# First attention of a two-layer block: projections spread over the slots, maxima turned in the products' bank, output bias as a weight row

## The chip, the cores and the metric

The kernel runs on one core of a Trainium2 chip. The metric is the device time of one execution in microseconds, the median of the runs of a kernel. Engines are called by the profile's names: PE is TensorE (matrix products; PEld its weight loads), DVE is VectorE, ACT is ScalarE, POOL is GpSimd, SP is SyncE, which here issues nearly all DMAs.

## The reference

Two layers, each a cross attention and a feed-forward stage, over 16 batches of 100 tokens of width 256. Only the first attention is touched by the change:

```
def _L0_xattn_ref(query, key_value, Wq, bq, Wk, bk, Wv, bv, Wo, bo):   # 16 heads of 16, 361 keys of width 192
    q = (query @ Wq + bq)       k = (key_value @ Wk + bk)       v = (key_value @ Wv + bv)    # split into heads
    attn = jnp.einsum('bhqd,bhkd->bhqk', q, k) * scale
    attn = jnp.clip(attn, -CLAMP, CLAMP)
    attn = jax.nn.softmax(attn, axis=-1)
    attn = jnp.where(jnp.any(jnp.isnan(attn)), jnp.asarray(1.0 / Nkv, attn.dtype), attn)
    x = jnp.einsum('bhqk,bhkd->bqhd', attn, v).reshape(B, Nq, Cq)
    return x @ Wo + bo
```

Its query is the layer norm of the tokens and its result is added to them. Behind it stand a mixture of experts, a second attention with quantised linears, and a gated cell; they take the rest of the time and stay as they are.

## The kernel before

It is written engine by engine: each engine's program is an order written out by hand, and the engines meet at semaphores. The attention runs batch by batch (`over_batches`: batches 0 and 1 written out, 2 to 11 in a loop of two batches a turn, 12 to 15 written out). A batch `b` is cut into eight slots `i`, one for each pair of heads, and `a_tensor`, `a_scalar`, `a_vector`, `a_gpsimd` give what each engine does in each slot; `a_sync` gives the DMA issues of a batch in their order.

In each slot TensorE does `t_tensor` (L551: the transposed scores of two heads of batch b, keys on the partitions, with the maximum subtracted by two extra rows, plus a floor column; banks 4 and 5), and then `s_tensor` (L532: the plain scores of two heads of batch b+1, banks 0 to 3 in turn). ScalarE takes the exponential of the first (`exp_scalar`, L558); VectorE takes the row maxima of the second (`s_vector`, L537) and clips the probabilities of the slot before (`clip_vector`, L567). Four times a batch `pv_tensor` (L581) multiplies four heads' probabilities by their values into bank 6, `OB_`, columns 0 to 399; a column of ones beside the values gives the softmax's denominator in partition 16 of each group of 32.

Between them lie the steps of later or earlier batches, all through one bank, 7, `UB_`, one after another, each waiting until the one before has been read: `k_tensor` (L379, two parts), `v_tensor` (L477, parts 0 and 1 of 12 and 6 products), `q_tensor` (L413), `y_tensor` (L623, the output product of batch b-2, read by `y_vector`, L633), and `m_tensor` (L506). The last turns eight heads' maxima, trimmed by `m_vector` (L500), so that they lie on rows; `m_scalar` (L512) and `m_low` (L516) split them into a high and a low half-precision part, and `rows_store` (L523) puts both as rows into the queries' tile, which `t_tensor` needs. `k_gpsimd` (L397), `q_gpsimd` (L430, L433) and `c_gpsimd` (L654) make the low parts of K, Q and the context on GpSimd, `on_gpsimd` (L617) scales the products by the inverted denominators. These come back by `inv_load` (L611), a DMA that spreads them over the partitions. `k_store` and `half_load` send K through DRAM into the layout of the scores.

The constant part of the output, bv·Wo + bo, is one row, `ybias`, made in the prologue; `x_bias_gpsimd` (L642) adds it to all tokens on GpSimd, four additions of 100x1024 in batches 0 and 1. Batches 14 and 15 also hold a guard for not-a-number (`guard_...`), whose sums and output product use `UB_` too.

Of the kernel before, what the change touches and what calls it, by code (L numbers as in the profile page):

```python
# [10 lines left out]
ALU = mybir.AluOpType  # L11
# [37 lines left out]
def build(nc, a, out):  # L49
    ctx = ExitStack()  # L50
    with ctx:
# [97 lines left out]
        def bias_row_tensor(pe, part):  # L149

            pe.wait_ge(wvo_in, 32)
            for k in range(2 * part, 2 * part + 2):
                pe.matmul(OB_[0:1, 0:C], bv_col[:, k:k + 1], w_in_["Wo_heads"][0][:, k, :], start=(k == 0), stop=False)
            if part == 1:
                pe.matmul(OB_[0:1, 0:C], ones_row[:, 0:1], bo_row[:, :], start=False, stop=True).then_inc(yb_mm, 1)
# [116 lines left out]
        least = sba("least", [T, H // 2])  # L272
# [13 lines left out]
        UH_ = UB_[:, :].bitcast(F16)  # L286
# [209 lines left out]
        def m_vector(v, b, p, half):  # L496
# [3 lines left out]
            v.scalar_tensor_tensor(m32c[:, :], m32[p][:, half * NP:(half + 1) * NP], CLAMP, least[:, :], ALU.min, ALU.max  # L500
                                   ).then_inc(m_c, 1)

        def m_tensor(pe, b, half, free):
            turn_free(pe, free)
            pe.wait_ge(m_c, 2 * b + half + 1)
            pe.transpose(UB_[0:NP, 0:T], m32c[:, :], ident[0:T, 0:T]).then_inc(m_mm, 1)  # L506

        def m_scalar(s, b, half):
# [3 lines left out]
            s.copy(mT[:, half, 0, :], UB_[0:NP, 0:T]).then_inc(m_h, 1)  # L512

        def m_low(v, b, half):
            v.wait_ge(m_h, 2 * b + half + 1)
            v.tensor_tensor(mT[:, half, 1, :], UB_[0:NP, 0:T], mT[:, half, 0, :], ALU.subtract).then_inc(m_l, 1)  # L516
# [52 lines left out]
        def pv_tensor(pe, b, p, g):  # L569
# [4 lines left out]
            if g == 0 and is_first(b):  # L574
                pe.wait_ge(yb_ev, 2)
# [43 lines left out]
        def y_tensor(pe, b, free):  # L619
            turn_free(pe, free)  # L620
            pe.wait_ge(o_n, b + 1)
            for k in range(HG):
                mm = pe.matmul(UB_[0:T, 0:C], on32[:, k * T:(k + 1) * T], w_in_["Wo_heads"][0][:, k, :], start=(k == 0),  # L623
                               stop=(k == HG - 1))
            mm.then_inc(y_mm0, 1)

        def y_vector(v, b):

            v.wait_ge(y_mm0, b + 1)
            if is_first(b):  # L630
                v.wait_ge(x_bias, LG)
# [29 lines left out]
        def a_tensor(pe, b, t, p):  # L661
            q = 1 - p
            for i in range(NP):
# [10 lines left out]
                if i % 2 and i >= 3:  # L674
                    pv_tensor(pe, b, p, (i - 3) // 2)
                if i == 1 and from_(b, 1):
                    pv_tensor(pe, b - 1, q, NQ - 1)
                if i == 0:
                    m_tensor(pe, b, 1, (k_32, 2 * b + 5) if has(b, 2) else (yb_ev, 3) if has(b, 1) else (y_x, b - 2))
                if i == 1 and has(b, 2):  # L680
                    k_tensor(pe, b + 2, p, 1, (m_l, 2 * b + 2))
                if i in (2, 3) and has(b, 1):
                    v_tensor(pe, b + 1, q, i - 2, (v_ev, 2 * b + 3) if i == 3 else
                             (k_32, 2 * b + 6) if has(b, 2) else (yb_ev, 4))
                if i == 4 and has(b, 1):
                    m_tensor(pe, b + 1, 0, (v_ev, 2 * b + 4))
                if i == 5 and has(b, 3):
                    q_tensor(pe, b + 3, q, (m_l, 2 * b + 3))
                if i == 6 and from_(b, 2):
                    y_tensor(pe, b - 2, (q_32, b + 4) if has(b, 3) else  # L690
                             (m_l, 2 * b + 3) if has(b, 1) else (m_l, 2 * b + 2))
                if i == 7 and has(b, 2) and not has(b, 3):
                    guard_sums_tensor(pe, (y_x, b - 1))
                if i == 1 and has(b, 1) and not has(b, 2):
                    guard_even_tensor(pe, (m_l, 2 * b + 2))
                if i == 7 and has(b, 3):
# [2100 lines left out]
```

## Time and profile before

| | |
|---|---|
| median of 3 runs | 946.31 us (946.12 to 947.51) |
| profiled execution | 947.37 us |
| its span, first to last instruction | 945.5 us |
| TensorE's granted clock, mean | 0.91 |
| busy: PE, DVE, ACT, POOL | 792.7, 708.9, 559.2, 298.9 us |

The profiled execution's own time is the span and what lies around it, 1.9 us. In the rows further down, a time is counted from the span's start. A row of the time order gives start, duration, engine, line, operation, the tile written and the tiles read, shapes, and in brackets the engine's idle time ahead of it with what ended it. Matrix products overlap: the distance between two starts, not the duration, is what one occupies.

### The profile page before, as it was taken

The numbers are of one execution on the slowest core, as the hardware profiler recorded it, in microseconds if no ns is written. First come the engines' busy times: TensorE is split into PE (matmuls) and PEld (weight loads), VectorE is DVE, ScalarE is ACT, GpSimd is POOL, SyncE is SP. The second block draws the span as 40 slices with busy tenths as digits, with TensorE's granted clock in tenths as the row PEclk, the third lists the DMA queues.
The fourth block names the chain that finished last, engine by engine and source line by source line (L and its number), as shares of the span: only waits on it lengthen the run. The fifth ranks groups of instructions, "written<-read, shape, count | busy, mean of one in ns | idle before, by whom it ended". The sixth has DMA issues, their size and how long they took to land.

```text
span 945.5 us, 22076 instructions
## 1 busy us (share of the span) xinstructions
PE 792.7 (84%) x8198; PEld 582.7 (62%) x8198; DVE 708.9 (75%) x1450; ACT 559.2 (59%) x1159; POOL 298.9 (32%) x258
## 2 busy tenths in 40 slices
PE   3777888889898768999889999997655999769994
PEld 2455666666665645777657777784213887459994
DVE  8678777877877888777476666654796998677866
ACT  6666666666665436634365555536897776673542
POOL 6166444444441506040232220002730221342400
PEclk9699999999999776999999999997557999789998
DMA  6423444344452246515076554455210000200002
GB/s 169 108 70 86 113 96 99 103 97 114 119 121 81 80 138 222 175 35 145 23 222 188 170 168 146 124 135 142 75 42 11 1 1 1 90 1 2 2 2 70
DMA packets 76898, 89.53 MB, mean 95 GB/s; under 512 B 22150, under 2 KB 64929, under 8 KB 76826
## 3 DMA queue, kind: packets, MB, share of 16 engines
q1 hardware_dynamic: 69994, 80.50, 30.6%
q0 software_dynamic: 6144, 7.42, 3.0%
q8 instruction: 45, 0.74, 0.3%
q10 hardware_dynamic: 688, 0.66, 0.3%
q14 instruction: 27, 0.22, 0.1%
HBM read 72.87 MB, written 15.43 MB: 93 GB/s over the span
## 4 chain that ended last, share of the span: by engine, by line
PE 53%; DVE 26%; ACT 9%; issue 8%; POOL 2%; DMA 1%; ACTq 0%; DVEq 0%; POOLq 0%
PE ps L1207 11%; PE ps L1194 10%; PE ps L581 4%; PE ps L379 3%; PE ps L477 3%; PE ps L551 3%; DVE p L567 3%; PE ps L623 3%; PE ps L532 2%; PE ps L2229 2%; DVE m L537 2%; PE ps L2240 2%; DVE pmax L1681 1%; ACT area L2039 1%; PE ps L1728 1%
## 5 line engine op out<-in xcount | busy, mean ns | idle before, releaser
L537 DVE TENSOR_REDUCE m<-ps 100x2 f32<-100x722 f32 x128 | 115.6, 904 | 51.6 <-PE ps L532 49.7
L558 ACT ACTIVATE p<-ps 128x800 f32<-128x800 f32 x128 | 106.8, 834 | 41.6 <-PE ps L551 38.6
L1256 ACT ACTIVATE hT<-ps,cols 128x500 f32<-128x500 f32 (+1 forms) x96 | 62.5, 651 | 103.3 <-PE ps L1194 103.1
L1263 DVE TENSOR_TENSOR hT_l<-hT,hT_h 128x500 f16<-128x500 f32 (+1 forms) x96 | 62.4, 652 | 59.1 <-ACT hT_h L1257 59.1
L567 DVE SCALAR_TENSOR_TENSOR p<-p 128x600 f32<-128x600 f32 x128 | 106.6, 834 | 0.0
L1207 PE MATMUL ps<-w_h,hT_h 128*125 128x256 f16 (+1 forms) x384 | 104.7, 273 | 1.8 <-DVE x L1303 1.2
L1207 PE MATMUL ps<-w_h,hT_l 128*125 128x256 f16 (+1 forms) x384 | 104.7, 273 | 0.0
L1207 PE MATMUL ps<-w_l,hT_h 128*125 128x256 f16 (+1 forms) x384 | 104.7, 273 | 0.0
L1099 POOL DMA_INDIRECT xe<-tokens,slot_of x32 | 43.2, 1349 | 151.4 <-PE ps L1217 102.1
L1194 PE MATMUL ps<-xe_h,w_h 128*128 128x500 f16 (+1 forms) x192 | 73.3, 382 | 15.8 <-DVE xe_l L1237 5.5
L551 PE MATMUL ps<-qs,ks 128*128 128x100 f16 x768 | 63.3, 212 | 14.7 <-ACT p L558 14.7
L1194 PE MATMUL ps<-xe_l,w_h 128*128 128x500 f16 (+1 forms) x192 | 73.0, 380 | 0.0
L1194 PE MATMUL ps<-xe_h,w_l 128*128 128x500 f16 (+1 forms) x192 | 72.6, 378 | 0.0
L551 PEld LDWEIGHTS ps<-qs,ks 128*128 128x128 f16 x768 | 51.1, 100 | 28.2 <-ACT p L558 20.1
L532 PE MATMUL ps<-ks,qs 128*100 128x361 f16 x256 | 62.9, 330 | 3.5 <-DMA qs<-q_parts 3.1
L397 POOL TENSOR_TENSOR kp<-k,kp 128x361 f16<-128x361 f32 x32 | 31.6, 989 | 98.8 <-ACT kp L393 98.8
L1257 ACT ACTIVATE hT_h<-ps,cols 128x500 f16<-128x500 f32 (+1 forms) x96 | 62.1, 647 | 0.0
L581 PE MATMUL ps<-p,v 128*32 128x100 f32 (+1 forms) x1536 | 48.7, 262 | 8.3 <-DVE p L567 8.0
L1207 PEld LDWEIGHTS ps<-w_h,hT_h 128*125 128x125 f16 (+1 forms) x384 | 50.9, 132 | 6.3 <-DVE hT_l L1263 1.4
L1207 PEld LDWEIGHTS ps<-w_l,hT_h 128*125 128x125 f16 (+1 forms) x384 | 50.9, 133 | 2.7
L1207 PEld LDWEIGHTS ps<-w_h,hT_l 128*125 128x125 f16 (+1 forms) x384 | 50.9, 133 | 0.0
L551 PE MATMUL ps<-qs,floor_k 128*128 128x100 f16 x256 | 50.7, 212 | 0.0
(348 smaller groups left out, 2101.6 us busy)
## 6 DMA issues: line engine op xcount, KB each, us to landing
sw<-in_L_ffn_w_dram SPq DMA_DIRECT2D x16, 512.0 KB, 6.8
sw<-in_L_ffn_w_dram SPq DMA_DIRECT2D x8, 1024.0 KB, 5.8
k_parts<-kp SPq DMA_DIRECT2D x32, 192.0 KB, 2.2
ks<-k_parts SPq DMA_DIRECT2D x32, 192.0 KB
stage<-in_L_xattn_W_f_dram SPq DMA_DIRECT2D x6, 1024.0 KB, 7.5
ctx_f<-in_ctxT_dram SPq DMA_DIRECT2D x16, 270.8 KB, 3.2
stage<-in_ctxT_dram SPq DMA_DIRECT2D x8, 541.5 KB, 8.6
area<-in_ctxT_dram SPq DMA_DIRECT2D x16, 270.8 KB, 6.1
```

Of the source, the lines that this page charges most:

```text
L532: mm = pe.matmul(bank[at + n][0:T, 0:KV], qs[p][:, h, :], ks[p][:, h, 0:KV], start=True, stop=True)
L537: v.tensor_reduce(m32[p][:, 2 * i:2 * i + 2], ps[0:T, at:at + 2, 0:KV], AX.X, ALU.max).then_inc(m_max, 1)
L551: mm = pe.matmul(bank[t_bank(i) + n][:, j * T:(j + 1) * T], keys, qs[p][:, h, :], start=(j == 0), stop=True, skip_group_check=True)
L558: s.activation(p32[:, i % HALF, :, :, :].rearrange("p j n t -> p n j t"), ps[:, t_bank(i):t_bank(i) + 2, 0:(KJ + 1) * T].rearrange("p n (j ...
L567: v.scalar_tensor_tensor(probs, probs, 1.0, low, ALU.min, ALU.max).then_inc(a_cv, 1)
L581: i = pe.matmul(OB_[HR * r:HR * (r + 1), g * T:(g + 1) * T], v32[p][0:m, j, h, :], p32[0:m, h // 2 % HALF, j, h % 2, :], start=(g == 0 and ...
L1099: g.indirect_dma_start(xe[e % 2][:, j, :], None, x_d, bass.IndirectOffsetOnAxis(ap=slot_of[:, 4 * e + j:4 * e + j + 1], axis=0)).then_inc( ...
L1194: i = pe.matmul(bank[2 + f % 2][:, 0:width(n)], w1p[ww][:, k, f * 128:(f + 1) * 128], xep[p][xx][:, k, 0:width(n)], start=(k == 0 and ww = ...
L1207: i = pe.matmul(bank[4 + j % 3][0:m, 0:C], hTp[p][hh][:, f, j * m:(j + 1) * m], w2p[of][ww][:, f, :], start=(f == 0 and hh == ww), stop=(f ...
L1256: s.activation(hT[:, f % 3, 0:m], bank[2 + f % 2][:, 0:m], ACT.Silu, bias=bias, scale=1.0 / WS)
L1257: s.activation(hTp[p][0][:, f, 0:m], bank[2 + f % 2][:, 0:m], ACT.Silu, bias=bias, scale=1.0 / WS).then_inc(f_s, 1)
L1263: v.tensor_tensor(hTp[p][1][:, f, 0:m], hT[:, f % 3, 0:m], hTp[p][0][:, f, 0:m], ALU.subtract).then_inc(f_l, 1)
```

## The change

- `over_batches` writes out batches 0 to 3 and loops over 4 to 11.
- K part 0 of batch b+2 moves from slot 7 of batch b-1 to slot 0 of batch b; V part 0 from slot 2 to 1, K part 1 from 1 to 2, Q from 5 to 4; V part 1 stays in slot 3; Y is cut in two halves, in slots 6 and 7; PV moves behind them in its slots. ScalarE's and GpSimd's orders follow.
- The maxima are turned into `MT_`, 100 columns of the products' bank behind the products, and no longer wait for `UB_`; instead TensorE waits for the maxima's low part (`m_l`) before the next PV.
- `ybias` is stored by a DMA from SyncE as row 16 of the output weight of head 0, where the denominator times its inverse, one, meets it. The additions on GpSimd go.
- On SyncE, the store of K part 1 comes after the loads of the next half, just before the maxima rows of batch b+1.
- In the prologue, Q of batch 2 moves up to slot 0, and the bias rows turn in `UB_`.
- The lower bound `least` of the trimming is one column, broadcast.

```diff
-        UH_ = UB_[:, :].bitcast(F16)
+        MT_ = OB_[0:H // 2, HG * T:(HG + 1) * T]
...
-            v.scalar_tensor_tensor(m32c[:, :], m32[p][:, half * NP:(half + 1) * NP], CLAMP, least[:, :], ALU.min, ALU.max
+            v.scalar_tensor_tensor(m32c[:, :], m32[p][:, half * NP:(half + 1) * NP], CLAMP, least[:, :].broadcast_to((T, NP)), ALU.min,
+                                   ALU.max
...
-        def m_tensor(pe, b, half, free):
-            turn_free(pe, free)
+        def m_tensor(pe, b, half):
             pe.wait_ge(m_c, 2 * b + half + 1)
-            pe.transpose(UB_[0:NP, 0:T], m32c[:, :], ident[0:T, 0:T]).then_inc(m_mm, 1)
+            pe.transpose(MT_, m32c[:, :], ident[0:T, 0:T]).then_inc(m_mm, 1)
...
-        def x_bias_gpsimd(g, n):
-            g.wait_ge(yb_ev, 2)
-            g.wait_ge(ln_xn, LB * (n + 1))
-            part = x[:, LB * n:LB * (n + 1), :]
-            g.tensor_tensor(part, part, ybias_b[:, None, :].broadcast_to((T, LB, C)), ALU.add).then_inc(x_bias, 1)
+        def bias_row_store(sp):
+
+            sp.wait_ge(yb_ev, 1)
+            sp.dma_start(w_in_["Wo_heads"][0][D:D + 1, 0, :], ybias[:, :]).then_inc(wvo_in, 16)
...
 def a_tensor(pe, b, t, p):
-                if i % 2 and i >= 3:
-                    pv_tensor(pe, b, p, (i - 3) // 2)
+                if i == 0:
+                    m_tensor(pe, b, 1)
+                if i == 0 and has(b, 2):
+                    k_tensor(pe, b + 2, p, 0, (y_x, b - 2) if from_(b, 3) else (q_32, b + 3) if from_(b, 1) else (yb_ev, 2))
+                if i == 1 and has(b, 2):
+                    v_tensor(pe, b + 1, q, 0, (k_32, 2 * b + 5))
+                if i == 1:
+                    pe.wait_ge(m_l, 2 * b + 2)
                 if i == 1 and from_(b, 1):
                     pv_tensor(pe, b - 1, q, NQ - 1)
-                if i == 0:
-                    m_tensor(pe, b, 1, (k_32, 2 * b + 5) if has(b, 2) else (yb_ev, 3) if has(b, 1) else (y_x, b - 2))
-                if i == 1 and has(b, 2):
-                    k_tensor(pe, b + 2, p, 1, (m_l, 2 * b + 2))
-                if i in (2, 3) and has(b, 1):
-                    v_tensor(pe, b + 1, q, i - 2, ...)
+                if i == 2 and has(b, 2):
+                    k_tensor(pe, b + 2, p, 1, (v_ev, 2 * b + 3))
+                if i == 3:
+                    pv_tensor(pe, b, p, 0)
+                if i == 3 and has(b, 1):
+                    v_tensor(pe, b + 1, q, 1, (k_32, 2 * b + 6) if has(b, 2) else (v_ev, 2 * b + 3))
                 if i == 4 and has(b, 1):
-                    m_tensor(pe, b + 1, 0, (v_ev, 2 * b + 4))
-                if i == 5 and has(b, 3):
-                    q_tensor(pe, b + 3, q, (m_l, 2 * b + 3))
+                    m_tensor(pe, b + 1, 0)
+                if i == 4 and has(b, 3):
+                    q_tensor(pe, b + 3, q, (v_ev, 2 * b + 4))
+                if i == 5 and has(b, 1):
+                    pe.wait_ge(m_l, 2 * b + 3)
+                if i == 5:
+                    pv_tensor(pe, b, p, 1)
                 if i == 6 and from_(b, 2):
-                    y_tensor(pe, b - 2, (q_32, b + 4) if has(b, 3) else ...)
+                    y_tensor(pe, b - 2, (q_32, b + 4) if has(b, 3) else ..., range(0, HG // 2))
+                if i == 7 and from_(b, 2):
+                    y_tensor(pe, b - 2, None, range(HG // 2, HG))
+                if i == 7:
+                    pv_tensor(pe, b, p, 2)
-                if i == 7 and has(b, 3):
-                    k_tensor(pe, b + 3, q, 0, (y_x, b - 1) if from_(b, 2) else (q_32, b + 4))
...
 def a_gpsimd(g, b, t, p):
-                if i == 1 and has(b, 2):
+                if i == 2 and has(b, 2):
                     k_gpsimd(g, b + 2, 0)
                 if i == 3:
-                    if has(b, 2):
-                        k_gpsimd(g, b + 2, 1)
-                    on_gpsimd(g, b - 2, p) if from_(b, 2) else x_bias_gpsimd(g, 2 * b)
+                    if from_(b, 2):
+                        on_gpsimd(g, b - 2, p)
+                if i == 4 and has(b, 2):
+                    k_gpsimd(g, b + 2, 1)
+                if i in (5, 7) and has(b, 3):
+                    c_gpsimd(g, b + 3, q, i // 2 - 2)
+                if i == 6 and has(b, 3):
+                    q_gpsimd(g, b + 3)
-                if i in (5, 6) and has(b, 3):
-                    c_gpsimd(g, b + 3, q, i - 5)
-                if i == 7 and has(b, 3):
-                    q_gpsimd(g, b + 3)
...
 def a_sync(sp, b, t, p):
             if has(b, 2):
-                k_store(sp, b + 2, t + 1, p, 1)
                 sp.wait_ge(a_s, NP * b + HALF)
                 half_load(sp, b + 2, p, 0)
+                k_store(sp, b + 2, t + 1, p, 1)
             if has(b, 1):
                 rows_store(sp, b + 1, q, 0)
```

## Rows read from the trace of the kernel before

**Rows 1.** stretches: length, busy PE, PEld, DVE, ACT, POOL, clock, DMA, GB/s

```profile
50.35:87.57 37.22, 28.70 (x418) 20.01 (x416) 32.43 (x40) 23.13 (x53) 27.70 (x16) 0.95 0.35 84
87.57:281.24 193.67, 172.64 (x2510) 121.63 (x2508) 152.99 (x242) 128.34 (x297) 86.79 (x79) 1.00 0.42 105
281.24:345.50 64.26, 49.98 (x698) 35.87 (x696) 53.79 (x94) 30.56 (x52) 18.31 (x10) 0.84 0.37 104
```

**Rows 2.** TensorE in time order, batch 6: start, us, what, [idle before]

```profile
163.05 0.28 PE L477 MATMUL ps<-Wv_h,ctxh 96*128 96x256 f16 x1 [0.17 <-ACT k L387]
...
165.78 0.32 PE L477 MATMUL ps<-Wv_h,ctxh 96*105 96x256 f16 x1
...
166.48 0.30 PE L551 MATMUL ps<-qs,ks 128*128 128x100 f16 x3
...
167.20 0.25 PE L506 MATMUL ps<-const,m32c 100*8 100x100 f32 x1
168.01 0.31 PE L551 MATMUL ps<-qs,ks 128*128 128x100 f16 x3 [0.56 <-ACT p L558]
...
169.00 0.72 PE L581 MATMUL ps<-p,v 128*32 128x100 f32 x24 [0.15 <-DVE p L567]
169.66 0.26 PE L413 MATMUL ps<-xnT,Wq_h 128*128 x2
...
170.20 0.30 PE L551 MATMUL ps<-qs,ks 128*128 128x100 f16 x3
...
171.31 1.97 PE L623 MATMUL ps<-Wo_heads_f,on 128*100 128x256 f32 x8 [0.28 <-ACT q L423]
173.11 0.29 PE L551 MATMUL ps<-qs,ks 128*128 128x100 f16 x3
...
174.53 0.33 PE L379 MATMUL ps<-ctxh,Wk_h 96*128 96x361 f16 x1
...
175.46 0.30 PE L551 MATMUL ps<-qs,ks 128*128 128x100 f16 x3
```

**Rows 3.** waits from 93 to 286 us: total us, times, longest

```profile
PE ps L551 <- ACT p L558: 9.7, 20, 0.6
```

**Rows 4.** ScalarE in time order, same batch

```profile
166.68 0.39 ACT L494 ACTIVATE v<-ps 105x256 f32<-105x256 f32 x1 [0.79 <-PE ps L477]
...
175.81 0.56 ACT L387 ACTIVATE k<-ps,bqk 128x361 f32<-128x361 f32 x1 [1.31 <-PE ps L379]
...
176.37 0.83 ACT L558 ACTIVATE p<-ps 128x800 f32<-128x800 f32 x1
```

**Rows 5.** VectorE in time order, same batch

```profile
168.87 0.24 DVE L516 TENSOR_TENSOR mT<-ps,mT 8x100 f16<-8x100 f32 x1
...
173.44 0.42 DVE L633 TENSOR_TENSOR x<-ps,x 100x256 f32 x1 [0.61 <-PE ps L623]
...
178.13 0.91 DVE L537 TENSOR_REDUCE m<-ps 100x2 f32<-100x722 f32 x1
178.95 0.78 DVE L567 SCALAR_TENSOR_TENSOR p<-p 128x600 f32<-128x600 f32 x1
```

**Rows 6.** all engines from 183.8 to 187.2 us

```profile
184.23 1.05 POOL L617 TENSOR_TENSOR on<-o,rden 128x400 f32<-128x400 f32 x1 [1.23 <-DMA rden<-inverse]
...
184.30 1.00 DVE L500 SCALAR_TENSOR_TENSOR m32c<-m,least 100x8 f32<-100x8 f32 x1
```

**Rows 7.** DMA issues of SyncE in time order, same batch

```profile
177.77 1.32 SPq L523 DMA_DIRECT2D qs<-mT  x2
179.19 0.57 SPq L611 DMA_DIRECT2D rden<-inverse  x1
```

**Rows 8.** GpSimd, with the bias addition on it

```profile
76.31 7.39 POOL L642 TENSOR_TENSOR x<-x,ybias_b 100x1024 f32<-100x1024 f32 x2
```

**Rows 9.** VectorE at the same moment

```profile
77.64 2.32 DVE L500 SCALAR_TENSOR_TENSOR m32c<-m,least 100x8 f32<-100x8 f32 x1
```

**Rows 10.** page, part 6: DMA issues, KB, us to landing

```profile
k_parts<-kp SPq DMA_DIRECT2D x32, 192.0 KB, 2.2
```

More of the change, by code:

```diff
@@ L271, in build @@
         floor_k = sba("floor_k", [128, AT], F16)
-        least = sba("least", [T, H // 2])
+        least = sba("least", [T, 1])
         p32 = sba("p32", [AT, QUAD, KJ + 1, 2, T])
@@ L673, in a_tensor @@
                     guard_flag_tensor(pe)
-                if i % 2 and i >= 3:
-                    pv_tensor(pe, b, p, (i - 3) // 2)
+                if i == 0:
+                    m_tensor(pe, b, 1)
+                if i == 0 and has(b, 2):
+                    k_tensor(pe, b + 2, p, 0, (y_x, b - 2) if from_(b, 3) else (q_32, b + 3) if from_(b, 1) else (yb_ev, 2))
+                if i == 0 and has(b, 1) and not has(b, 2):
+                    guard_sums_tensor(pe, (y_x, b - 2))
+                if i == 1 and has(b, 2):
+                    v_tensor(pe, b + 1, q, 0, (k_32, 2 * b + 5))
@@ L694, in a_tensor @@
-                if i == 1 and has(b, 1) and not has(b, 2):
-                    guard_even_tensor(pe, (m_l, 2 * b + 2))
-                if i == 7 and has(b, 3):
-                    k_tensor(pe, b + 3, q, 0, (y_x, b - 1) if from_(b, 2) else (q_32, b + 4))
+                if i == 1 and has(b, 1) and not has(b, 2):
+                    guard_even_tensor(pe, (yb_ev, 3))
+                if i == 2 and has(b, 2):
+                    k_tensor(pe, b + 2, p, 1, (v_ev, 2 * b + 3))
+                if i == 2 and has(b, 1) and not has(b, 2):
+                    v_tensor(pe, b + 1, q, 0, (yb_ev, 4))
@@ L701, in a_scalar @@
             for i in range(NP):
-                if i == 0 and has(b, 2):
-                    k_scalar(s, b + 2, p, 0)
                 if i == 1:
                     m_scalar(s, b, 1)
-                if i == 2 and has(b, 2):
-                    k_scalar(s, b + 2, p, 1)
-                if i in (3, 4) and has(b, 1):
-                    v_scalar(s, b + 1, q, i - 3)
+                if i in (1, 3) and has(b, 2):
+                    k_scalar(s, b + 2, p, i // 2)
+                if i == 1 and has(b, 1) and not has(b, 2):
+                    guard_sums_scalar(s)
+                if i == (2 if has(b, 2) else 3) and has(b, 1):
+                    v_scalar(s, b + 1, q, 0)
+                if i == 4 and has(b, 1):
+                    v_scalar(s, b + 1, q, 1)
                 if i == 5 and has(b, 1):
@@ L714, in a_scalar @@
                 exp_scalar(s, b, i)
-                if i == 0 and has(b, 1) and not has(b, 2):
-                    guard_sums_scalar(s)
+                if i in (1, 3) and has(b, 2):
+                    k_high(s, b + 2, i // 2)
                 if i == 2 and not has(b, 1):
@@ L720, in a_scalar @@
                     o_scalar(s, b - 1, q)
-                if i in (0, 2) and has(b, 2):
-                    k_high(s, b + 2, i // 2)
-                if i in (4, 5) and has(b, 3):
-                    c_scalar(s, b + 3, q, t + 1 + p, i - 4)
+                if i in (4, 6) and has(b, 3):
+                    c_scalar(s, b + 3, q, t + 1 + p, i // 2 - 2)
         def a_vector(v, b, t, p):
@@ L736, in a_vector @@
                     m_low(v, b + 1, 0)
-                if i == 7 and from_(b, 2):
-                    y_vector(v, b - 2)
                 if has(b, 1):
@@ L744, in a_vector @@
                     guard_row_vector(v)
+                if i == 7 and from_(b, 2):
+                    y_vector(v, b - 2)
                 if i >= 1:
@@ L980, in over_batches @@
         def over_batches(eng, body):
-            for b in range(2):
-                body(b, 0, b)
-            with eng.Fori(1, B // 2 - 2) as t:
+            for b in range(4):
+                body(b, b // 2, b % 2)
+            with eng.Fori(2, B // 2 - 2) as t:
                 for p in range(2):
```

58 lines of the change are left out of this document (27 added, 31 removed).

## Prediction

> **What bounds the kernel now.** I read the stretches first, because the diff touches only the first attention: 50.4 to 345.5 us of a span of 945.5 [rows 1]. The eleven batches 2 to 12 take 193.67 us, 17.61 each. TensorE is the busiest there (172.6 us by modelled ends), VectorE next (153.0), at full clock (1.00). Neither is full. So the view that matters is TensorE in time order over one batch [rows 2], read for the distance between starts, which is what an operation really occupies, and for the idle times with their releasers.
>
> Names: T is the transposed scores of a pair of heads, S the scores of the next batch's pair, PV a group of products, K and V the projections by part, M a transpose of maxima, Y the output product; i numbers the eight slots, each of which begins with T and S. From the starts [rows 2]: T and S together 0.72 (166.48 to 167.20), PV 0.66, V1 0.70, Q 0.54, Y 1.80, K 0.93, V0 2.73 - 0.72 - 0.66 = 1.35, M some 0.1 (its modelled 0.25 overlaps). A batch is 8 x 0.72 + 4 x 0.66 + 1.35 + 0.70 + 0.54 + 1.80 + 2 x 0.93 + 0.2 = 14.85 us. The other 2.75 us are waits. The largest kind is T for the exponential of the slot before (9.7 us in 20 waits, [rows 3]): T writes the two banks that this exponential reads (0.83 us, [rows 4]), so a slot needs about 1 us of other work behind T. Slots 0 and 4 have S and M alone: 0.72 + 0.1 from 167.20 gives 167.29, and T starts at 168.01. The second kind is the one bank through which K, M, V, Q and Y turn: Y waits at 171.31 for Q's reading, and after a K the reading is over only at 176.37 + 0.1, 1.0 us after K's last issue at 175.46, while T and S fill 0.72.
>
> **The change part by part.**
>
> *Spreading the projections.* No operation is added or dropped, so the 14.85 stays; only waits change. I walk the new order with time zero at T of slot 4, which is the end of V1.
> Slot 4: V1's reading starts 0.2 later and takes 0.39 [rows 4], the exponential 0.83 behind it ends near 1.5. TensorE has T, S, M and now Q, 1.36: wait 0.15 in place of 0.7.
> Slot 5: T and S end at 2.25. PV1 now waits for the low part of the maxima, since these lie in the products' bank. Before, that ran 168.87 to 169.11 [rows 5], 2.63 after T of slot 4: wait 0.4 in place of 0.3. Queued behind PV1 are T and S of slot 6, and VectorE's reductions behind those.
> Slots 6 and 7: Y is cut in halves of 0.90, each behind T and S, with PV2 last. Q's reading is over, so the 0.4 before Y goes, and each exponential has 0.36 + 0.90 beside it: no wait.
> Slot 0: VectorE reads Y (0.42), clips (0.70) and trims the maxima (under 0.24) from 0.3 after Y's end (173.11 to 173.44) [rows 5], behind a reduction of 0.82 (178.13 to 178.95); TensorE has PV2, T and S, 1.38, so M waits 0.2. K0 follows, and the exponential is covered (0.36 + 0.1 + 0.2 + 0.93).
> Slot 1: V0 waits 0.3 for K0's reading, as before. Slot 2: K1 waits for V0's reading behind PV3, T and S, 1.38: none. Slot 3: PV0 waits some 0.1 for VectorE, V1 none.
> Waits 0.15 + 0.4 + 0.2 + 0.3 + 0.1 = 1.15; a batch of 16.0 us.
>
> *What speaks against it: GpSimd.* Its order changes to K-low 0, output scaling, K-low 1, context, Q, context, and each now falls later against VectorE. The trace shows the two excluding each other: GpSimd's scaling runs 184.23 to 185.28 and VectorE's tiny trimming of 8 columns, started at 184.30, takes 1.00 us and ends at 185.30 [rows 6], where the low maxima's 100 columns take 0.24 [rows 5]. The clips read SBUF just so, and I take them as exposed too. The scaling starts when its row broadcast lands, 5.0 us after its issue (179.19 to 184.23, [rows 6, 7]), which puts it at about 0.2 of my frame, K-low 1 at 1.4 to 2.3, so that the clip of slot 4, due at 1.7, waits 0.6 and with it the low maxima, PV1 and everything behind; with 0.1 for a clip beside Q's parts a batch is 16.7. My value is 16.5, nearer the port's figure than the clean one since VectorE's own work is 13.9 us of a batch (153.0 / 11, [rows 1]) and it has little slack. Bounds 16.0 and 17.2 (two more such collisions of 0.25 on the path). Eleven batches: 11 x (17.6 - 16.5) = 12.1 us, bounds 17.6 and 4.4.
> The Trainium skill has this exclusion in "SBUF — State Buffer", section "Who interferes with whom": a VectorE instruction with two SBUF inputs and a GpSimd one that reads SBUF block each other fully, in issue order. By that rule, the trace agrees for the trimming (1.00 us beside the 1.05 us scaling), and the sum is the 16.7 of the clips held; without it, it is the 16.0.
>
> *The bias as a weight row.* Four additions of 3.7 us leave GpSimd in batches 0 and 1 (two of them are the 7.39 of [rows 8]). They held VectorE: a trimming took 2.32 [rows 9], M and all behind it late. The two batches take 37.22 us [rows 1], 18.6 each, though they have no Y. After it each is 16.5 less Y's 1.8, of which the exponential's wait gives back some 0.7: 15.4. Gain 37.2 - 30.8 = 6.4, bounds 5 and 8. The new row is one DMA of 1 KB from SyncE's queue in the prologue, behind the first maxima rows; it is needed first by batch 2's Y, and what queues behind it there is a zero row's store and the loads of batch 1, not due before batch 0's slots; the product with the denominator's row costs nothing, as 128 weight rows are multiplied anyway. `least` shrunk to a column leaves an instruction of 100x8: nothing, bounds -0.1 and +0.1 a batch, inside the range.
>
> *Prologue.* Q (0.54) and K (0.93), with the wait between them for Q's reading, leave the place before batch 0's first T; Q and its reading move ahead of the third transposed group, on the way to the first maxima, and T cannot start before the first maxima rows have landed. Taking 0.5 of the 1.47 as given back so, the net is -1.0, bounds -2.5 (with the wait) and +0.5 (Q's own time twice over, none of the rest gained).
>
> *Tail.* Batch 13 gains some 0.9 (its Q and slot 4), batch 14 some 0.6: the even-row sums move from slot 7 of 13 to slot 0 of 14, where their reading is hidden by T, S and PV3, but V0 still waits for VectorE there. Batch 15 is bound by VectorE and GpSimd's long additions: 0. Together -1.5, bounds -2.5 and 0. Four bodies instead of two before the loop: one turn of the loop fewer, nothing. From 345.5 us on nothing is touched, and it moves as a whole.
>
> Sum: -1.0 - 6.4 - 12.1 - 1.5 = -21.0. The profiled execution took 947.37, which gives 926.4; the median of the runs shown is 946.31, and 946.3 - 21.0 = **925.3 us**.
>
> **Rivals.**
> *TensorE alone bounds it* (the collisions fall under reductions, which read PSUM and are not held): 16.0 a batch, 17.6 + 7.4 + 2 + 2 = 29, so 917. For: in the old order most collisions did that. Against: the scaling and K-low 1 now stand just before the clip of slot 4.
> *VectorE and GpSimd become the bound*: clips behind context and Q parts in slots 5 to 7 make trimming late in slot 0, and K0 waits. 17.2 to 17.5 a batch, the bias gain left: 2 to 4 + 6 = 9, so 937. For: VectorE has 16.5 - 13.9 = 2.6 us of slack, and GpSimd is busy for 7.9 us of a batch, waits for the port among them (86.8 / 11, [rows 1]).
> *The opposite sign: SyncE's queue.* The maxima rows of the next batch are now issued behind the store of K-low 1, which waits for GpSimd, which waits for the scaling's broadcast, itself issued behind rows that need M after T of slot 0. From T of slot 0 (175.46): broadcast issued 3.7 later, landed 8.8, scaling 1.05, K-low 1.0, two clips in the way 1.5, store 0.4, rows 1.32: 14.0, plus their landing, before the next batch's first T. A landing of 2.2, as the K parts' [rows 10], gives 16.2 and is hidden; one of 5.0, as the broadcast's, gives 19.0 and costs 11 x 1.4 = 15, less 7 from the bias and prologue: 954. It decides against the change from a landing of about 4.4 (18.4 a batch). Against: each of these rows is one partition's, the broadcast fills 128.
> *No change*: batches gain under 0.2 each by some queue and the bias stall had been hidden. [rows 9] speaks against.
>
> **How the numbers follow.** Forecast (919 to 932) 0.55; TensorE alone 0.17; VectorE with GpSimd 0.20; no change 0.03; slower 0.05. The first three are faster: 0.92. A change of 0.2% (1.9 us) is about what a measurement of this kernel can tell from none. The range runs from 915 (all low bounds) to 937, which leaves out half of the third case, the last two, and a little below 917.
>
> **What the profile would show.** Right: batches of about 16.5 us from V0 to V0; T of slots 0 and 4 no longer waiting 0.5 for the exponential; new waits of PV1 for VectorE's low maxima in slot 5 and of M in slot 0; no addition on GpSimd and no 2.3 us trimming in batches 0 and 1; some trimmings or clips stretched by GpSimd. Wrong: T of slot 0 waiting for the maxima's DMA (the queue), K0 waiting for the context's low part, or VectorE without idle time between its operations. The forecast fails above all if I mis-time the scaling by half a microsecond, since that decides which engine takes the port first.

## The result, and the profile after

The changed kernel takes 934.4 us (median of 4 runs, 934.1 to 938.1) against 946.9 (946.1 to 947.9) for the kernel before, measured beside it: ratio 0.9876, 95% interval 0.9849 to 0.9903. It is faster by 12.5 us. I had forecast 21, so the sign holds and 934.4 lies in the full range of 915 to 937; but it lies above the 919 to 932 that I had given as the forecast proper, in the stretch of the rival in which VectorE and GpSimd bound. The profiled execution is the slowest of the four (938.05, span 936.2); what it holds more than the others lies behind the attention and is named below.

The stretches of the kernel after, cut as [rows 1] (batches 0 and 1, then 2 to 12, each from the first T to the first T):

```profile
48.64:79.29 30.65, 27.10 (x416) 19.00 (x417) 26.50 (x39) 23.00 (x54) 14.17 (x12) 1.00 0.40 102
79.29:265.81 186.52, 173.50 (x2513) 122.04 (x2509) 161.12 (x244) 129.22 (x297) 106.12 (x78) 1.00 0.44 109
```

Read the first figure behind each window. Batches 0 and 1 take 30.65 us instead of 37.22: 6.6 gained, 6.4 forecast. The eleven batches take 186.52 instead of 193.67: 16.96 each, not 16.5, so 7.15 gained of the 12.1. TensorE's busy time hardly moved (173.5 against 172.6), as it should, but VectorE's rose from 153.0 to 161.1 and GpSimd's from 86.8 to 106.1 with no operation more: these two hold each other up more than before.

The rest of the sum, from the starts of T of slot 0: the attention's first batch begins 1.7 us earlier, batches 13 and 14 together give back 0.5 (T of batch 15 starts 14.95 earlier than before), batch 15 gives back 1.5 more, and at the end of the attention, which is the end of its last output product, 13.4 are left.

What TensorE waits for, 93 to 280 us (waits above 0.15 us); columns: total us, times, longest:

```profile
PE ps L506 <- DVE m32c L500: 8.2, 18, 0.6
PE ps L477 <- ACT k L387: 1.9, 8, 0.2
PE ps L579 <- DVE mT L516: 1.8, 5, 0.4
PE ps L551 <- ACT p L558: 0.5, 1, 0.5
```

The wait of [rows 3], T for the exponential, is gone from the eleven batches, as forecast (the one left belongs to batch 13). In its place stands M (L506) for the trimming, and most of it in slot 0: over the eleven batches M waits there every time, 5.7 us together (0.2 to 0.9 each), and in slot 4 in eight of them, 3.3 us (0.41 or 0.42 each). V0 (L477) for K0's reading waits 0.24 in eight batches; PV1 (L579) for the low maxima waits 0.2 to 0.4, but in five batches only. Batch 4 in time order, and the first slots of batch 5, show how M's wait in slot 4 arises. TensorE, answering to [rows 2]:

```profile
122.80 0.30 PE L551 MATMUL ps<-qs,ks 128*128 128x100 f16 x3
...
124.04 0.25 PE L506 MATMUL ps<-const,m32c 100*8 100x100 f32 x1 [0.41 <-DVE m32c L500]
124.23 0.34 PE L413 MATMUL ps<-xnT,Wq_h 128*128 x2
...
124.96 0.30 PE L551 MATMUL ps<-qs,ks 128*128 128x100 f16 x3
...
127.08 1.08 PE L623 MATMUL ps<-Wo_heads_f,on 128*100 128x256 f32 x4
...
131.50 0.25 PE L506 MATMUL ps<-const,m32c 100*8 100x100 f32 x1 [0.15 <-DVE m32c L500]
...
133.68 0.28 PE L477 MATMUL ps<-Wv_h,ctxh 96*128 96x256 f16 x1 [0.23 <-ACT k L387]
```

VectorE beside it, answering to [rows 6]:

```profile
122.29 0.77 DVE L567 SCALAR_TENSOR_TENSOR p<-p 128x600 f32<-128x600 f32 x1
122.98 1.00 DVE L500 SCALAR_TENSOR_TENSOR m32c<-m,least 100x8 f32<-100x8 f32 x1
123.91 0.90 DVE L537 TENSOR_REDUCE m<-ps 100x2 f32<-100x722 f32 x1
124.73 0.77 DVE L567 SCALAR_TENSOR_TENSOR p<-p 128x600 f32<-128x600 f32 x1
```

and GpSimd:

```profile
121.83 2.13 POOL L615 TENSOR_TENSOR on<-o,rden 128x400 f32<-128x400 f32 x1 [2.93 <-DMA rden<-inverse]
123.92 2.32 POOL L397 TENSOR_TENSOR kp<-k,kp 128x361 f16<-128x361 f32 x1
126.19 1.93 POOL L652 TENSOR_TENSOR ctxl<-ctx_f,ctxh 96x361 f16<-96x361 f32 x1
```

The broadcast has landed at 121.83 and the scaling is recorded from there, 2.13 us long, where it takes 1.04 undisturbed; so it did its own work only from about 122.9, when the clip was ending. That the clip at 122.29 was not held (0.77), though the scaling is recorded 0.46 ahead of it, I can't explain from these rows: a start on record does not by itself tell which of the two goes first. Then the trimming, 8 columns and 0.16 us of work, is behind the scaling: 1.00 us. M waits 0.41, and Q, T of slot 5 and all behind it start that much later. The next clip (124.73) takes its plain 0.77, with K-low 1 stretched to 2.32 around it. This is the collision that the prediction had taken from [rows 6], with the roles the other way: I had made the clip pay and the trimming free.

The same happens in slot 0 of seven of the eleven batches, beside the context's second low part. Both operations are drawn out, and it is the short one that TensorE waits for, 0.5 to 0.9 us; in the four batches in which the trimming takes its 0.16, M waits 0.2 to 0.35. From batch 10:

```profile
215.22 1.77 POOL L652 TENSOR_TENSOR ctxl<-ctx_f,ctxh 96x361 f16<-96x361 f32 x1
216.18 0.84 DVE L500 SCALAR_TENSOR_TENSOR m32c<-m,least 100x8 f32<-100x8 f32 x1
...
217.07 0.25 PE L506 MATMUL ps<-const,m32c 100*8 100x100 f32 x1 [0.64 <-DVE m32c L500]
```

In SyncE's queue the maxima rows follow the store of K-low 1 at once, as the rival of the opposite sign had it:

```profile
126.26 0.39 SPq L404 DMA_DIRECT2D k_parts<-kp  x1
126.74 1.36 SPq L523 DMA_DIRECT2D qs<-mT  x2
```

T of slot 0 starts at 130.51 without a wait, 2.4 us after the rows' issue has ended (128.10): they land in at most that, well under the 4.4 from which that rival decides.

### The profile page after: what moved, and what is told of

Same layout as the page of the kernel before. It is cut to its first block, busy times and chain, and to the rows that moved or that the text cites. A ratio compares the mean times of both kernels' runs of the same rounds, so it can differ in the third digit from the quotient of the medians.

```text
span 936.2 us, 21941 instructions
## 1 busy us (share of the span) xinstructions
PE 795.3 (85%) x8198; PEld 584.8 (62%) x8198; DVE 711.5 (76%) x1450; ACT 559.5 (60%) x1159; POOL 309.4 (33%) x254
## 4 chain that ended last, share of the span: by engine, by line
PE 44%; DVE 28%; issue 9%; ACT 7%; DMA 7%; POOL 4%; SPq 1%; DVEq 0%; ACTq 0%; POOLq 0%
PE ps L1217 11%; PE ps L1204 8%; DVE p L567 4%; PE ps L379 3%; DVE m L537 3%; PE ps L477 2%; PE ps L2239 2%; PE ps L551 2%; DVE m32c L500 2%; PE ps L532 2%; PE ps L579 2%; PE ps L2250 2%; DVE pmax L1691 1%; ACT area L2049 1%; DMA rden<-inverse 1%
## 5 line engine op out<-in xcount | busy, mean ns | idle before, releaser
L397 POOL TENSOR_TENSOR kp<-k,kp 128x361 f16<-128x361 f32 x32 | 46.7, 1459 | 62.6 <-ACT kp L393 62.6
L551 PEld LDWEIGHTS ps<-qs,ks 128*128 128x128 f16 x768 | 49.0, 99 | 22.9 <-ACT p L558 10.1
L579 PE MATMUL ps<-p,v 128*32 128x100 f32 (+1 forms) x1536 | 47.6, 258 | 8.3 <-DVE p L567 4.6
L579 PEld LDWEIGHTS ps<-p,v 128*32 128x32 f32 (+1 forms) x1536 | 33.4, 112 | 27.5 <-issue 10.8
```

Source lines behind the costliest of these rows:

```text
L397: g.tensor_tensor(kp[:, 1, c, 0:KV], k32[c][:, :], kp[:, 0, c, 0:KV], ALU.subtract).then_inc(k_l, 1)
L551: mm = pe.matmul(bank[t_bank(i) + n][:, j * T:(j + 1) * T], keys, qs[p][:, h, :], start=(j == 0), stop=True, skip_group_check=True)
L579: i = pe.matmul(OB_[HR * r:HR * (r + 1), g * T:(g + 1) * T], v32[p][0:m, j, h, :], p32[0:m, h // 2 % HALF, j, h % 2, :], start=(g == 0 and ...
```

## The experiments

All times are compared with the kernel before on the same chip, whose median there was 950.9, 951.3 and 949.9 us in the three groups below. The changed kernel itself took 935.46 (ratio 0.9846, 0.9808 to 0.9885) with the second group and 936.22 (0.9862, 0.9828 to 0.9897) with the third, 17.01 and 17.00 us for each of the eleven batches. "Mean batch" is that quantity throughout, read from one trace. It is steadier than the totals: in the three traces of the changed kernel it is 16.96, 17.01 and 17.00, while the part behind the attention, whose work no edit changes, takes 598 to 609 us in the fourteen traces. The first group has no changed kernel beside it; there the ratios are held against the 0.9876 (0.9849 to 0.9903) above.

**The same kernel again, beside the second and third group**

> The changed kernel itself, as the base of the three beside it on the same chip. Batches 2 to 12 at 16.96 us each as in its first profile, the first T before 49 us; total 12 us below the kernel before on this chip.

> The changed kernel itself, as the base of the three beside it on the same chip: 16.96 to 17.01 a batch, 0.985 of the kernel before.

**First group: what each part is worth**

*The bias row alone*, in the old order:

```diff
...
-                    on_gpsimd(g, b - 2, p) if from_(b, 2) else x_bias_gpsimd(g, 2 * b)
+                    if from_(b, 2):
+                        on_gpsimd(g, b - 2, p)
...
-                if i == 4 and not from_(b, 2):
-                    x_bias_gpsimd(g, 2 * b + 1)
...
+            bias_row_store(sp)
...
```

> The kernel before with the bias as a weight row and nothing else of the change. Theory (the additions hold VectorE in batches 0 and 1): their two batches, 37.2 us before, fall to 2 x 16.5 (17.6 less Y's 1.8, 0.7 given back by the exponential's wait) = 33.0, so 942.5 us. Rival (in the old order other waits stand where the held trimming stood): under 1.5 us of gain, 945.5 or more.

943.76 us, ratio 0.9921 (0.9891 to 0.9952). The two batches take 31.80 us instead of 37.22, 5.4 less, more than either figure given; the eleven stay at 17.60. The additions' harm is to batches 0 and 1 alone.

*The order alone*: the changed kernel with the additions back.

> The changed kernel with the four additions back on GpSimd, in slots 3 and 4 of batches 0 and 1, and no weight row. If bias and order are independent, it loses against the changed kernel what the kernel before gains by the weight row, about 4 us: 938.5. Rival (the spread order leaves less room, so the additions hold more): 5.5 us or more, 940 and above.

943.63 us, ratio 0.9917 (0.9889 to 0.9945). Mean batch 16.90, batches 0 and 1 37.63: in the spread order the additions cost 7.0 us, where they cost 5.4 in the old one. The rival is right in the trace; in the total, the intervals of this kernel and the changed one overlap. TensorE's waits there, and the windows (columns as in [rows 1]), show why:

```profile
57.74 0.25 PE L506 MATMUL ps<-const,m32c 100*8 100x100 f32 x1 [1.34 <-DVE m32c L500]
...
63.63 0.62 PE L579 MATMUL ps<-p,v 128*32 128x100 f32 x17 [1.26 <-DVE p L567]
...
67.78 0.33 PE L379 MATMUL ps<-ctxh,Wk_h 96*128 96x361 f16 x1 [1.95 <-POOL ctxl L653]
```

```profile
56.00:64.00 8.00, 4.55 (x88) 3.04 (x90) 8.00 (x10) 5.32 (x14) 7.95 (x5) 1.00 0.31 94
64.00:70.00 6.00, 3.59 (x43) 2.22 (x35) 3.21 (x6) 1.56 (x4) 3.70 (x2) 0.84 0.26 52
70.00:76.00 6.00, 5.70 (x66) 3.73 (x64) 3.63 (x5) 4.02 (x10) 3.95 (x2) 0.87 0.24 64
```

GpSimd is full (7.95 of 8 us), so the context's low part, which it now makes later, is late for K0 (1.95), a wait of its own in this order. And behind a stretch in which TensorE worked 4.55 of 8 us, its granted clock is 0.84 and 0.87. The kernel before has the same, 0.95 over its two batches [rows 1] and 0.72 between 62 and 68 us; the changed kernel and the one with the bias row alone have 1.00.

*No trimming*: TensorE turns the maxima as they are. This leaves out the bounding of the maxima at plus and minus the clamp.

```diff
...
-        def m_tensor(pe, b, half):
-            pe.wait_ge(m_c, 2 * b + half + 1)
-            pe.transpose(MT_, m32c[:, :], ident[0:T, 0:T]).then_inc(m_mm, 1)
+        def m_tensor(pe, b, p, half):
+            pe.wait_ge(m_max, NP * b + HALF * (half + 1))
+            pe.transpose(MT_, m32[p][:, half * NP:(half + 1) * NP], ident[0:T, 0:T]).then_inc(m_mm, 1)
...
```

> The changed kernel, leaving out the trimming of the maxima to plus and minus 40000: TensorE turns the untrimmed maxima and waits for the reduction itself. Theory (the trimming, held by GpSimd's scaling in slot 4 and by the context part in slot 0, is what made a batch 16.96 and not 16.5): a batch near 16.3, so 7 us less than the changed kernel, 927. Rival (VectorE's throughput bounds): only its own 0.16 and 0.3 twice a batch, at most 3 us less, 931 or more.

928.86 us, ratio 0.9802 (0.9732 to 0.9871), mean batch 16.56: 0.40 less than the changed kernel's first trace, between the two expectations, which allow 0.27 at most (the rival) and 0.66 (the theory). The ratio's interval overlaps the changed kernel's, so this rests on the batch. M's waits for the trimming are gone: between starts of T, slot 4 is 0.4 and slot 0 0.3 shorter. Part of what they held comes back as others, PV1's above all (slot 5 is 0.2 longer):

```profile
PE ps L571 <- DVE mT L508: 4.1, 12, 0.4
PE ps L379 <- POOL ctxl L644: 3.4, 7, 0.6
PE ps L477 <- ACT k L387: 1.9, 8, 0.2
PE ps L543 <- DMA qs<-mT: 1.8, 3, 0.6
```

*The broadcast's load issued earlier*, so that the scaling would begin before the place where it collides:

```diff
                 q_store(sp, b + 2, t + 1, p)
+            if b >= 2 and has(b, 1):
+                inv_load(sp, b - 2)
...
             rows_store(sp, b, p, 1)
-            if b >= 2 and has(b, 1):
-                inv_load(sp, b - 2)
```

> The changed kernel with the load of the inverted denominators issued 3.7 us earlier, right behind the store of Q's parts, so that GpSimd's scaling is over in slot 2. Theory (that scaling holds the trimming in slot 4): the trimming's 1.00 us goes or is held by K-low 1 instead, which then starts near it: between 0 and 0.4 us a batch, 929 to 934. Rival (the scaling's place is without weight, the chain through the maxima rows' queue sets the batch): the queue is busy 0.6 earlier and nothing else moves: 934.4 plus or minus 0.7.

943.0 us, ratio 0.9917 (0.9887 to 0.9946), mean batch 17.27: slower than the changed kernel by the batch, 0.3; the ratios' intervals just overlap. Neither figure was right, since a third thing happened. M no longer waits, but T of slot 4 does, in all eleven batches (0.3 to 2.0 us), for the rows of the maxima that now follow the broadcast. SyncE's issues and then TensorE, batch 10:

```profile
215.05 0.58 SPq L609 DMA_DIRECT2D rden<-inverse  x1
...
217.50 1.34 SPq L523 DMA_DIRECT2D qs<-mT  x2
```

```profile
225.60 0.43 PE L551 MATMUL ps<-qs,ks 128*128 128x100 f16 x3 [2.03 <-DMA qs<-mT]
```

The rows land at 225.6, 6.8 us after their issue ended, behind the broadcast's issue at 215.05; over the eleven batches it is 5.0 to 6.8. In the changed kernel the same rows go ahead of the broadcast, T comes 5.0 to 5.9 after the end of their issue, and it never waits: so they land within that there, but how much sooner the rows don't tell. The four loads of K and Q parts stand ahead of them in both kernels. Behind this wait of 2 us TensorE's granted clock is 0.64 between 226 and 230 us.

**Second group: which of the two engines goes first**

*The trimming as an operation with constants* (one tensor input instead of two):

```diff
-            v.scalar_tensor_tensor(m32c[:, :], m32[p][:, half * NP:(half + 1) * NP], CLAMP, least[:, :].broadcast_to((T, NP)), ALU.min,
-                                   ALU.max
-                                   ).then_inc(m_c, 1)
+            v.tensor_scalar(m32c[:, :], m32[p][:, half * NP:(half + 1) * NP], CLAMP, -CLAMP, ALU.min,
+                            ALU.max).then_inc(m_c, 1)
```

> The changed kernel with the trimming as a tensor-scalar instruction: both bounds as constants, one input instead of two. Theory (the shared port is taken for the second SBUF input, and that alone holds the trimming): no trimming above 0.3 us, a batch of 16.6 as without any trimming, 4 us less than the changed kernel. Rival (this form is held by GpSimd as well): 1.00 us trimmings stay, a batch of 16.96, no difference.

937.96 us, ratio 0.984 (0.9797 to 0.9883), mean batch 16.98. The rival is right: it is held just the same. Of its 32 executions 18 take 0.5 us or more, up to 1.04; of the 32 in the changed kernel 19 do (8 near 1.00, 11 near 0.8), the others in both 0.15 to 0.17.

*The scaling waits for the trimming*:

```diff
                 if i == 3:
                     if from_(b, 2):
+                        if has(b, 1):
+                            g.wait_ge(m_c, 2 * b + 3)
                         on_gpsimd(g, b - 2, p)
```

> The changed kernel in which GpSimd's scaling waits for the trimming of slot 4. Theory (it is the order of the two that costs): the trimming of slot 4 takes 0.16, M of slot 4 no longer waits 0.41, GpSimd's chain moves back some 0.2: a batch of 16.7, 3 us less. Rival (GpSimd's operations then hold the clips behind instead, and PV1 waits the longer): 16.9 to 17.0, no difference.

935.4 us, ratio 0.9839 (0.9783 to 0.9895), mean batch 16.78, 0.23 less than the changed kernel beside it; the theory had 16.7. The same place as above, now in this kernel, all engines:

```profile
123.29 0.16 DVE L500 SCALAR_TENSOR_TENSOR m32c<-m,least 100x8 f32<-100x8 f32 x1
123.72 1.03 POOL L615 TENSOR_TENSOR on<-o,rden 128x400 f32<-128x400 f32 x1 [4.52 <-DVE m32c L500]
...
125.78 0.47 PE L579 MATMUL ps<-p,v 128*32 128x100 f32 x12 [0.32 <-DVE mT L516]
```

The trimming takes 0.16, M has no wait in slot 4, and the scaling, with 4.52 us idle ahead of it instead of 2.93, takes 1.03 in place of 2.13: GpSimd loses 0.5. The waits of slot 0 remain (9 of M, where the changed kernel beside it has 20), and PV1's grow from 1.0 to 3.7 us in 93 to 280: part of the rival. In the total, these 2.5 us can't be told from the changed kernel (0.9839 and 0.9846, with intervals of 0.8%).

*Constants, and the context's second part ahead of Q's on GpSimd*, to free slot 0; beside the edit with constants above:

```diff
-                if i in (5, 7) and has(b, 3):
-                    c_gpsimd(g, b + 3, q, i // 2 - 2)
-                if i == 6 and has(b, 3):
+                if i in (5, 6) and has(b, 3):
+                    c_gpsimd(g, b + 3, q, i - 5)
+                if i == 7 and has(b, 3):
                     q_gpsimd(g, b + 3)
```

> The trimming as a tensor-scalar instruction, and the context's second low part ahead of Q's parts on GpSimd. Theory (without the held trimming, K0 in slot 0 waits for that context part by 0.6 every second batch, as the kernel without trimming showed): 0.3 a batch less than the kernel with the tensor-scalar trimming alone, 16.3, 3 us less than that. Rival (another wait takes its place): 16.5 or more.

943.2 us, ratio 0.9899 (0.9851 to 0.9948), mean batch 17.14: the rival, another wait, is right. The waits of TensorE, 93 to 280:

```profile
PE ps L550 <- DMA qs<-mT: 9.3, 10, 1.6
PE ps L578 <- DVE mT L515: 3.3, 10, 0.4
PE ps L622 <- POOL on L614: 2.0, 2, 1.0
```

M hardly waits any more (0.4 once), and T waits for the maxima rows instead. The next group shows where that comes from.

**Third group: the queue**

*The maxima rows ahead of the store of K-low 1*:

```diff
-                k_store(sp, b + 2, t + 1, p, 1)
             if has(b, 1):
                 rows_store(sp, b + 1, q, 0)
+            if has(b, 2):
+                k_store(sp, b + 2, t + 1, p, 1)
```

> The changed kernel with the maxima rows of the next batch issued ahead of the store of K part 1. Theory (in the changed kernel the rows have landed when T of slot 0 comes, so the queue does not bound it): a batch of 16.96 as before, total within 1 us of the changed kernel. Rival (the queue of my prediction's slower case already costs part of it): 16.7 or less.

933.47 us, ratio 0.9822 (0.9792 to 0.9851) beside 0.9862 (0.9828 to 0.9897) for the changed kernel, intervals that overlap. Ten of the eleven batches are as in the changed kernel (16.3 to 17.4); one, batch 12, took 21.32, which makes a mean of 17.28. In that one K0 waits 2.00 for the context's low part, and the granted clock is 0.50 in the four microseconds behind. TensorE was 1.3 us further on there than in the changed kernel (T of slot 0 at 247.90 for 249.19), GpSimd was not, and its operation took longer: 248.96 to 251.27, for 248.82 to 250.60. The other ten batches average 16.87, for 16.99 and 17.04 in the changed kernel (first and last trace), and stay above the rival's 16.7; in the changed kernel T never waits for the rows. So the queue does not bound it.

*GpSimd's wait, the context's order and the rows first, together* (the three edits shown above):

> Three edits on the changed kernel: scaling behind the trimming of slot 4, the context's second low part ahead of Q's parts on GpSimd, maxima rows ahead of the store of K part 1. Theory (held trimmings cost 0.23 in slot 4 and some 0.2 in slot 0 of every second batch, and the waits of T for the rows, which came with the context order, stood behind the store): no T waits for a DMA, trimmings at 0.16, a batch of 16.4 to 16.6, 5 us below the changed kernel. Rival (T still waits for the rows, because their landing is late by itself behind other transfers): 17 or more.

944.65 us, ratio 0.9939 (0.9912 to 0.9967), mean batch 17.43, which is the rival's figure. The theory fell. The issue of the rows, and T, batch 5:

```profile
131.58 1.36 SPq L523 DMA_DIRECT2D qs<-mT  x2
```

```profile
135.69 0.31 PE L551 MATMUL ps<-qs,ks 128*128 128x100 f16 x3 [0.87 <-DMA qs<-mT]
```

The rows' issue ended at 132.94 and they had landed at 135.69, 2.75 later. Two things add up. The issue comes late, 4.3 us after T of slot 4, where with the rows alone moved it came 2.1 to 2.4 after (batches 2 to 9), though the store of K-low 1 is no longer ahead of it. And the landing is longer in some batches: 1.6 to 3.3 us in the seven in which T of slot 0 waits, for at most 2.4 in the changed kernel. For the second part the rival is right. What SyncE's queue itself waits for, 93 to 280, in the changed kernel:

```profile
SPq L404 <- POOL kp L397: 25.9, 21, 2.4
SPq L453 <- DMA k_parts<-kp: 20.4, 11, 3.3
...
SPq L442 <- POOL qp L433: 2.9, 7, 0.4
```

and in this one:

```profile
SPq L453 <- DMA k_parts<-kp: 39.0, 11, 4.3
SPq L442 <- POOL qp L433: 22.7, 11, 4.0
```

With the context's second part ahead of Q's on GpSimd, the store of Q's parts (L442) waits 22.7 us in place of 2.9 (11.1 in the kernel with constants), and behind it in the queue stand the loads, the rows and the broadcast. So the trimming was freed in slot 0 by an order that delays all of the next batch's transfers. GpSimd's wait and the store's place I can't separate from it here, and why some rows land later stays open.

*The store of K part 1 back ahead of the loads*, the one move on SyncE's queue that the change makes, undone:

```diff
             if has(b, 2):
+                k_store(sp, b + 2, t + 1, p, 1)
                 sp.wait_ge(a_s, NP * b + HALF)
                 half_load(sp, b + 2, p, 0)
-                k_store(sp, b + 2, t + 1, p, 1)
```

> The changed kernel with the store of K part 1 back ahead of the loads of the next half. Theory (K-low 1 is over only at the end of slot 5 now, so the store, the four loads and the maxima rows behind it all come 2 to 3 us later, and T of slot 0 waits for the rows): a batch of 17.8 to 18.5, slower than the changed kernel by 9 to 17 us. Rival (the loads and rows still land in time): no difference.

955.71 us, ratio 1.0065 (1.0041 to 1.0088), mean batch 18.10: inside the theory's 17.8 to 18.5, and slower than the kernel before. The total is 19.5 above the changed kernel's, beyond the theory's 17; the eleven batches hold 12 of it. SyncE's order, then T, then the waits from 93 to 280:

```profile
127.65 0.38 SPq L404 DMA_DIRECT2D k_parts<-kp  x1
128.12 0.42 SPq L455 DMA_DIRECT2D ks<-k_parts  x1
...
129.90 1.36 SPq L523 DMA_DIRECT2D qs<-mT  x2
```

```profile
133.22 0.31 PE L551 MATMUL ps<-qs,ks 128*128 128x100 f16 x3 [1.26 <-DMA qs<-mT]
```

```profile
PE ps L551 <- DMA qs<-mT: 18.8, 10, 3.2
```

The store waits for K-low 1, and the loads behind it, four issues and 1.8 us, come between it and the maxima rows. This is the mechanism of my rival of the opposite sign, found here and not in the changed kernel: the changed kernel avoids it by the order of three calls on SyncE.

## Why the prediction was right in sign and short in size

*Batches 0 and 1: right, the size partly by luck.* 6.6 gained where I had 6.4. The additions' removal gives 5.4 in the old order and 7.0 in the new one, so part of it belongs to both edits together. A piece of it is one I had not named: the lower granted clock behind the additions' stalls (0.72 between 62 and 68 us). And the 6.4 was built on the 16.5 below: with the measured 16.96 the same sum gives 5.5.

*Batches 2 to 12: the step that failed is the 16.5 us a batch*, in the paragraph on GpSimd, measured 16.96 (17.0 in both repeats). Its mechanism was right: VectorE and GpSimd exclude each other, and TensorE waits for it. Its place was not. I put the scaling at 0.2 behind T of slot 4, let K-low 1 hold the clip of that slot by 0.6, and left both trimmings free. Laid beside the walk by the starts on TensorE, mean of the eleven batches:

| | walk | measured |
|---|---|---|
| slot 0, T to K0 (S and M between) | 1.02 | 1.53 |
| K0 and slots 1 to 3 | 7.79 | 7.99 |
| slot 4, T to Q (S and M between) | 0.82 | 1.23 |
| slot 4, Q to T of slot 5 | 0.69 | 0.70 |
| slot 5 | 1.78 | 1.61 |
| slots 6 and 7 | 3.90 | 3.89 |
| batch | 16.0 | 16.96 |

So M costs 0.5 more than walked in slot 0, mostly where the trimming is held, and 0.4 more in slot 4, where I had no wait for it. The 0.2 in slots 1 to 3 is no wait: T and S take 0.85 ahead of K1 and PV0, not 0.72. PV1, which I had let wait 1.0 with the collision, waits 0.2, less than even the clean walk's 0.4. In slot 4 the scaling starts between 0.97 ahead of T and 0.06 behind it in the eight batches with a held trimming, and 0.5 to 0.9 behind T in the three in which the trimming takes 0.16. In six of the eight that is over half a microsecond off my 0.2, the failure that I had named. It isn't the broadcast: that lands 8.7 us after T of slot 0 (batch 4), as my 3.7 and 5.0 have it. It is T of slot 4 that comes later, after 9.7; and the walk's own slots 0 to 3 add up to 8.8, so my figures put the scaling at -0.1 and not at 0.2.

Without the trimming a batch is 0.40 shorter and lands on 16.56; with GpSimd waiting for it in slot 4 alone, 0.23 shorter. So of the 0.46 missed, leaving the trimming out gives back 0.40. That this is near my 16.5 is chance: other waits have come in there, K0's for the context's low part and T's for the rows, which neither the walk nor my collision had. The rival "TensorE alone", 16.0, is ruled out by the 16.96 and by M's waits for held trimmings. The rival in which VectorE and GpSimd bound is right in part: it had late trimmings in slot 0, which are here, and K0's wait for the context, which isn't; and at 16.96 the batch stays below its 17.2.

In the Trainium skill, "SBUF — State Buffer", section "Who interferes with whom", a VectorE instruction with two SBUF inputs and a GpSimd one that reads SBUF block each other in issue order. By that rule the trimming behind an already issued scaling takes the scaling's time; the traces agree, 1.00 us in the changed kernel and 0.16 where GpSimd is made to wait. The clip of batch 4, not held behind a scaling recorded 0.46 ahead of it, does not follow from the recorded starts.

*Prologue: 1.7 for my 1.0, not shown to be the change's.* The kernel with the bias row alone, whose prologue is the old one but for a DMA, starts its first T at 48.63 as well, and the other kernels start between 47.1 and 49.9.

*Tail: wrong, by 3.5 us.* It gives back 2.0 where I had 1.5 gained. I had 0.9 and 0.6 for batches 13 and 14; batch 13 takes 17.18 where it took 16.35, a loss of 0.8 (17.18 and 16.55 in the two repeats), and batch 14 18.35 for 18.69. K part 0 of the last batch, which stood in slot 7 of batch 12, now stands in slot 0 of batch 13: counting the prologue's K as a gain and batch 13 as if it did no more work, I had counted one K of 0.93 twice.

Batch 15 loses 1.5, forecast 0, of which 1.3 before the denominator's product: up to there TensorE waits 3.6 us for clips where it waited 2.1, and a scaling takes 2.40 where it took 1.27. But in the two repeats that part is 0.1 shorter and 1.4 longer than before, while the whole loss is 2.2 and 1.7. So the loss is real and its cause is not found; that the two engines hold each other there too is not shown.

*Behind the attention: 0 forecast.* Of the 13.4 the median keeps 12.5; how the executions without a trace divide it isn't known. The profiled execution (938.05 against 947.37, 9.3 less) lost 4.1 there, nearly all at one wait of ScalarE for a DMA of the experts' weights at 470.7 us, 6.3 us where it was 2.4; it is 2.6 and 3.1 in the repeats. The other three executions have spans 3.5 to 4.0 shorter, so that delay is likely this execution's own.

*Sum*: 1.7 + 6.6 + 7.15 - 0.5 - 1.5 (batch 15 to the attention's end) = 13.4. The 7.6 us missed at that point are 5.0 of the batch term and 3.5 of the tail, less 0.9 that the first two terms gave beyond their forecast.

**What stays open.** What made GpSimd's context part of one batch take 2.31 us when the rows went first, why rows behind the broadcast land so late, which of the two engines goes first when their starts lie close, and where batch 15 loses. The wait of PV1 for the low maxima was not tried alone, since the maxima lie in the products' bank and no other bank is free. No version tried is shown to beat the changed kernel: GpSimd's wait for the trimming gives 0.23 a batch in the trace, and the totals can't tell it; the kernel without the trimming leaves out a part of the function.

## What to carry to other kernels

When two engines exclude each other, the short operation can pay for the long one: here 0.16 us became 1.00, and it stood on the critical chain. So write both engines' orders side by side around the moment at which a transfer releases one of them, move that moment by half a microsecond either way, and ask which short operation would then stand behind. A wait on the engine with slack was the cheap remedy here (GpSimd lost 0.5 and TensorE gained 0.23 a batch), though it freed one of two places and the total did not show it. And when steps are spread over slots, check the DMA queue for a store that waits on the delayed engine: here its place among SyncE's issues decides between some 13 us gained and 6 lost.

## What the runs showed of the hardware that was not expected

- Two DMAs of 1.6 KB each, the maxima rows, land within 2.4 us of their issue's end in slot 0 of the changed kernel. Those of slot 4 take 5.0 to 6.8 us when the broadcast to 128 partitions is issued some 2.5 us ahead of them in the same queue; issued ahead of it, they are there when T comes, after 5.0 to 5.9 us.
- A VectorE operation on 8 columns with one tensor input in the buffer and constants is held by GpSimd just as the form with two is: 0.16 us free, up to 1.04 held, in 18 executions of 32 (19 of 32 with two).
- Which of two colliding operations goes first can't be read from the recorded starts alone: a clip recorded 0.46 us behind the scaling's start took its plain 0.77, and the scaling 2.13 for 1.04.
- TensorE's granted clock fell from 2.4 GHz to its lower level, 1.2, behind stalls inside an otherwise full stretch: 0.50 for four microseconds behind a wait of 2.00 us, 0.64 behind one of 2.03, 0.84 in the six behind eight in which it worked 4.55. So such a wait costs more than its own length: the batch with the wait of 2.00 took 21.32 where it takes 16.62 in the changed kernel. In the kernel with constants and the context reordered, with waits of up to 1.6 us, it stayed at 1.00 between 93 and 260 us.
